# Eleven of the late units of a two-layer stage from one fp32 product to three fp32r products, with the low half made by VectorE out of PSUM

## The reference

```python
xm = x * cmask                                  # channels past a count are zero
h = gelu(einsum('bct,bch->bht', xm, W_sess[id]) + b_sess[id])     # 256 hidden
o = (einsum('bht,hs->bst', h, W2) + b2) * tmask                   # 128 out, masked in time
w_q = fp8_e4m3(weight * 448 / max|weight|)                        # 2048 x 2048
o_q = fp8_e5m2(o * 57344 / max|o|)
out = x + (o_q @ w_q.T) / scales + bias
```

## Time and profile before

| | |
|---|---|
| median of 3 runs | 832.65 us (832.58 to 834.17) |
| the profiled execution | 834.57 us, of which 832.8 us are the span of the profile |
| TensorE | 824.1 us busy, 99% of the span, 98% of the chain that ended last |
| VectorE / ScalarE / GpSimd | 479.5 / 345.8 / 511.8 us busy |
| granted TensorE clock | 1.00 |
| stage one ends, stage two starts | about 382 us after the start of the span |

### The profile page before, as it was taken

One profiled execution on the slowest core, in us unless ns is written; L12 is line 12 of the kernel. 1 busy time (PEld: TensorE's weight loads), 2 busy tenths in 40 slices (PEclk: granted clock), 3 DMA queues, 4 the chain that ended last, 5 costly groups with the idle time before them and its releaser, 6 DMA issues.

```text
span 832.8 us, 10134 instructions
## 1 busy us (share of the span) xinstructions
PE 824.1 (99%) x3521; PEld 481.6 (58%) x3568; DVE 479.5 (58%) x499; ACT 345.8 (42%) x372; POOL 511.8 (61%) x238
## 2 busy tenths in 40 slices
PE   9999999999999999999999999999999999999998
PEld 6777777776767676765444444444444444444444
DVE  5989899888888888888553333323232323232322
ACT  6899999988898888883200000000000000000000
POOL 2899999889999999995983242424242424232322
PEclk9999999999999999999999999999999999999999
DMA  7888999878777777656974768686868686868682
GB/s 257 300 324 311 387 322 348 307 283 305 298 270 301 302 289 287 249 202 230 308 293 124 272 219 279 212 281 210 283 214 282 212 281 213 283 214 280 213 251 107
DMA packets 75008, 220.77 MB, mean 265 GB/s; under 512 B 37594, under 2 KB 40930, under 8 KB 55778
## 3 DMA queue, kind: packets, MB, share of 16 engines
q1 hardware_dynamic: 74080, 219.30, 74.1%
q10 hardware_dynamic: 898, 1.09, 0.4%
HBM read 143.04 MB, written 69.21 MB: 255 GB/s over the span
## 4 chain that ended last, share of the span: by engine, by line
PE 98%; issue 0%; DMA 0%; DVE 0%; ACTq 0%; ACT 0%
PE ps_h L1071 53%; PE ps_h L980 22%; PE ps_o L995 11%; PE ps_o L1011 8%; PE ps_o L1007 4%; DMA counts_i<-in__lenS 0%; PE ps_h L1047 0%; PE ps_o L934 0%; PE ps_o L1071 0%; PE ps_o L980 0%; PE ps_o L940 0%; PE ps_o L1065 0%; ACTq L650 0%; PE ps_h L1052 0%; DVE o_and_max L881 0%
## 5 line engine op out<-in xcount | busy, mean ns | idle before, releaser
L1071 PE MATMUL ps_h<-wqT,x_sb 128*128 128x512 bf16 x1877 | 411.3, 378 | 2.4 <-ACT x_sb L702 0.2
L1071 PEld LDWEIGHTS ps_h<-wqT,x_sb 128*128 128x128 fp8e5 x1920 | 187.7, 98 | 224.4 <-ACT x_sb L702 0.3
L528 POOL TENSOR_TENSOR xl<-x_sb,xh 128x1024 fp32r<-128x1024 f32 x62 | 149.6, 2413 | 17.5 <-ACT xh L607 17.5
L980 PE MATMUL ps_h<-xh,whl 128*128 128x512 f32 x508 | 151.6, 419 | 0.4
L569 POOL TENSOR_TENSOR x_sb<-x_sb,bias_sb 128x2048 f32<-128x2048 f32 (+1 forms) x15 | 66.7, 4445 | 131.7 <-DMA x_sb<-in_x 131.7
L569 POOL TENSOR_TENSOR h<-h,bias_sb 128x2048 f32<-128x2048 f32 (+1 forms) x15 | 66.6, 4442 | 123.0 <-DMA h<-in_x 123.0
L881 DVE SCALAR_TENSOR_TENSOR o_and_max<-ps_h,scales,h 128x512 f32<-128x512 f32 (+1 forms) x59 | 44.0, 746 | 136.2 <-PE ps_h L1071 136.2
L881 DVE SCALAR_TENSOR_TENSOR o_and_max<-ps_h,scales,x_sb 128x512 f32<-128x512 f32 x59 | 44.2, 750 | 133.4 <-PE ps_h L1071 133.4
L980 PEld LDWEIGHTS ps_h<-xh,whl 128*128 128x128 f32 x508 | 95.0, 189 | 41.9 <-issue 21.9
L765 DVE SCALAR_TENSOR_TENSOR o_and_max<-ps_o,b_sb,steps 128x1024 f32<-128x1024 f32 (+1 forms) x65 | 82.2, 1264 | 29.0 <-PE ps_o L1011 27.2
L755 DVE TENSOR_TENSOR hl<-ps_h,hh 128x1024 fp32r<-128x1024 f32 x63 | 76.8, 1219 | 15.1 <-ACT ps_h L614 15.1
(11 more groups left out here) (101 smaller groups left out, 657.6 us busy)
## 6 DMA issues: line engine op xcount, KB each, us to landing
x_sb<-in_x SPq DMA_DIRECT2D x44, 1024.0 KB, 5.6
masked_out<-o_and_max SPq DMA_DIRECT2D x32, 1024.0 KB, 6.6
o_in<-masked_out SPq DMA_DIRECT2D x32, 1024.0 KB, 8.9
out<-o_and_max SPq DMA_DIRECT2D x27, 1024.0 KB, 5.1
wqT<-in_L_ffn_weight SPq DMA_DIRECT2D x23, 684.0 KB, 8.2
wt<-in_L_ffn_weight SPq DMA_DIRECT2D x40, 384.0 KB, 5.4
h<-in_x SPq DMA_DIRECT2D x14, 1024.0 KB, 7.2
whl<-split_w SPq DMA_DIRECT2D x18, 256.0 KB, 5.9
```

Of the source, the lines that this page charges most:

```text
L528: pool.tensor_tensor(xl[:, u % 2, :], x_cols(u), xh[:, u % 2, :].bitcast(fp32), ALU.subtract)\
L980: mm = nc.tensor.matmul(to[:, cols], whl[:, b % SLOTS_W, rows], xs[:, u % 2, cols], start=(k == 0), stop=(k == 2))
L1071: mm = nc.tensor.matmul(bank, q[:, k // 2, :, k % 2], wq[:, n, k, cols], start=(k == 0), stop=(k == KT - 1))
```

## The change

Unit 27 joins `SPLIT_H1`. Eleven units (30, 33, ... 60, `SPLIT_BEHIND`) get three fp32r products in `project1` in place of one fp32 product. ACT writes their high half to SBUF and the full gelu back into PSUM (in place of one gelu to SBUF), and DVE makes the low half out of `ps_h[:, 1, :]`, where the same work for units 2 to 27 is POOL's. The next `hidden(u+1, 1)` then waits for DVE too. `QUANT` becomes 27, so that 34 chunks are early and 9 late; the constants of chunk 34 are made in the last iterations of stage one, ACT scales chunk 36 ahead of the copies of the turned batch, and DVE's late chunks stand behind groups 2, 4, 5, 6 and 7 (before: 4, 5, 6, 7).

```diff
-    SPLIT_H1 = [u for u in range(2, 27)]
+    SPLIT_H1 = [u for u in range(2, 28)]
+
+    SPLIT_BEHIND = [u for u in range(30, UNITS - 2, 3)]
...
-    QUANT = SCANS + 2
+    QUANT = SCANS + 3
...
-    CHUNK_BEHIND = range(4, 12)
+    CHUNK_BEHIND = (2, 4, 5, 6, 7)
...
+        hh1_behind = sb_at("hh1_behind", [P, 2, UNIT], fp32r, h1_at)
+        hl1_behind = sb_at("hl1_behind", [P, UNIT], fp32r, raw_at)
...
-            for i in late[0:2]:
+            for i in late[0:3]:
                 round_chunk(i)
             pool.wait_ge(x2_loaded[1], 16)
             add_bias(x2[1], FRONT)
-            for i in late[2:6]:
+            for i in late[3:7]:
                 round_chunk(i)
...
+                if u in SPLIT_BEHIND:
+                    act.activation(hh1_behind[:, u % 2, :], ps_h[:, 1, :], ACT.Gelu, bias=hbias[:, 1, b:b + 1])
+                    act.activation(ps_h[:, 1, :], ps_h[:, 1, :], ACT.Gelu, bias=hbias[:, 1, b:b + 1])\
+                       .then_inc(h1_gelu, 1)
+                    return
...
+            scale_chunk(EARLY_CHUNKS + 2)
+
             for k in range(CUTS):
                 act.wait_ge(q_turned, k + 1)
...
+            def split_h1_behind(u):
+
+                dve.wait_ge(h1_gelu, u + 1)
+                if u == SPLIT_BEHIND[0]:
+                    dve.wait_ge(wl_later, DIRECT - UPB)
+                dve.tensor_tensor(hl1_behind[:, :], ps_h[:, 1, :], hh1_behind[:, u % 2, :].bitcast(fp32), ALU.subtract)\
+                   .then_inc(hl1_behind_ready, 1)
...
                     mask_o(u - 1, start, 0, slice(0, UNIT))
+                    if u in SPLIT_BEHIND:
+                        split_h1_behind(u)
...
+                if 0 <= u - QUANT - 1 < EARLY_CHUNKS:
+                    exponents(u - QUANT - 1)
                 if 0 <= u - QUANT - 1 < EARLY_CHUNKS + 1:
-                    exponents(u - QUANT - 1)
-                if 0 <= u - QUANT - 1 < EARLY_CHUNKS:
                     round_at(u - QUANT - 1)
                 if u + 1 < UNITS:
                     split_h_rest(u + 1)
+                if u - QUANT - 1 == EARLY_CHUNKS - 1:
+                    exponents(EARLY_CHUNKS)
...
             late = range(EARLY_CHUNKS, CHUNKS)
-            round_at(late[0])
             quantize(1, 1, True, slice(0, T))
...
                     pe.wait_ge(h1_gelu, u)
+                    if u - 1 in SPLIT_BEHIND:
+                        pe.wait_ge(hl1_behind_ready, SPLIT_BEHIND.index(u - 1) + 1)
...
+                elif u in SPLIT_BEHIND:
+
+                    for j, (w, hs) in enumerate(((w2l1, hh1_behind[:, u % 2, :]), (w2h1, hh1_behind[:, u % 2, :]),
+                                                 (w2h1, hl1_behind))):
+                        for cols in halves:
+                            mm = nc.tensor.matmul(ps_o[:, u % 2, cols], w[:, :], hs[:, cols],
+                                                  start=False, stop=(j == 2))
```

More of the change, by code:

```diff
@@ L126, in adaln_ffn @@
         x_sb = sb("x_sb", [P, 2, T], fp32)
+        raw_at = -(-nc.sbuf_base // 32) * 32
         raw = sb("raw", [P, SLOTS_W, HID], fp32)
+        assert SLOTS_W * HID == UNIT
         whl = sb("whl", [P, SLOTS_W, 2 * HID], fp32r)
@@ L137, in adaln_ffn @@
         hl = sb("hl", [P, 2, UNIT], fp32r)
+        h1_at = -(-nc.sbuf_base // 32) * 32
         h1 = sb("h1", [P, 2, UNIT], fp32)
@@ L236, in adaln_ffn @@
         hl1_ready = sem("hl1_ready")
+        hl1_behind_ready = sem("hl1_behind_ready")
         hl_ready = sem("hl_ready")
@@ L582, in _ @@
             add_bias(x2_more[0], FRONT)
-            for i in late[6:]:
+            for i in late[7:]:
                 round_chunk(i)
@@ L705, in _ @@
             for i in range(EARLY_CHUNKS + 2, CHUNKS):
-                scale_chunk(i)
+                if i > EARLY_CHUNKS + 2:
+                    scale_chunk(i)
                 if UNITS - QUANT + 2 <= i + 3 < CHUNKS:
@@ L902, in _ @@
                        .then_inc(y_ready, 1)
-                if y in CHUNK_BEHIND and 4 + CHUNK_BEHIND.index(y) < len(late):
+                if y in CHUNK_BEHIND:
                     i = late[4 + CHUNK_BEHIND.index(y)]
```

## The result

The changed kernel is slower: a ratio of 1.0098 to the kernel before, 95% interval 1.0086 to 1.011. Its six runs have a median of 842.6 us (840.43 to 842.76), the kernel before 833.48 (832.58 to 834.17) over six. The profiled execution took 842.63 us, against 834.57. The forecast was 841.2 us, with a range of 839 to 845.5.

The account below looks back on a forecast made before the run. PE's own sequence bounds the kernel, but in eleven units it would come to wait for DVE's `hl`: 8.9 - 0.34 = +8.6 us, from the 832.65 us median 841.2 us. Range 839 to 845.5 us, to hold 8 times in 10.

Parts of the forecast that it names:

- Which wait would end last: PE in the eleven units: the wait for `hl` decides; the new wait at `hidden(u+1, 1)` for the subtract lies inside it.
- The slack: DVE's chain to `hl` before the change: could end only 0.19 us later before delaying PE's next `hidden`.
- The addition: DVE's chain from `mask_o` to `hl`: the new subtract lengthens it by 1.02 us, at most 1.26.
- The restart: PE after a real wait: its xl group starts 0.15 + 1.00 = 1.15 us after `hl` ends.
- A unit: Each of the eleven units: PE's next xl group later by 0.83 us (odd) or 0.79 us (even), 8.9 us in all.
- PE's saving is inside the wait: `project1` of the eleven units: the 0.34 us saved by three products only brings PE to the wait sooner.
- Unit 27: Three products with POOL making the low half and no chunk worked on in that iteration: -0.34 us.
- The number: Whole kernel: +8.6 us, giving 843.1 us for an execution like the profiled one and 841.2 us from the 832.65 median.
- The late part: Late chunks after stage one: cost 0, or +3 us if the cover fails; ACT has 3.3 us before the first copy.
- The followed-forward times of POOL: POOL's late chunks in stage two: third `add_bias` forecast at about 415.2, before the change 415.05.
- The 3 us of cover: Stage two, group 6: DVE waits for POOL's third `add_bias`, PE wants that bank at about 422.4, slack 3 us.
- The rule on four passes of true fp32: Trainium skill's rule for PE's fp32 products: dropping one pass would save 0.43 us a unit, where the rows give 0.34.

Follow-up runs that it names:

- e_subtract_after_scan: Changed kernel with DVE's subtract behind scan_o instead of ahead of it: median 844.47 us, ratio 1.0136 to the kernel before.
- d_no_subtract: Changed kernel without the subtract and PE's wait for it, the third product taking the high half again: median 831.24 us, ratio 0.9964 to the kernel before.
- b_twice: Changed kernel plus a second DVE instruction of the subtract's size, an unread reduce, in the eleven units: median 855.02 us, ratio 1.025 to the kernel before.
- a_no_behind: Changed kernel with SPLIT_BEHIND empty, keeping unit 27 on three products, QUANT 27 and nine late chunks: ratio 0.9995 to the kernel before.
- c_fp32_product: Changed kernel with one fp32 product of the high half in the eleven units, low half made but left out: median 842.56 us, ratio 1.0098.
- f_scan_last: Changed kernel with scan_o behind split_h_rest from unit 29 on: median 833.19 us, ratio 0.9993 to the kernel before; 829.4 us was expected.
- h_scan_last_every2: Changed kernel with scan_o behind split_h_rest and every second unit from 30 (16, not 11) on three products: median 831.97 us, ratio 0.9977.
- j_no_subtract_scan_last: Changed kernel, scan_o behind split_h_rest except in stage one's last two iterations, no subtract or wait for it, high half counted again: median 828.63 us, ratio 0.9936.

## Why the prediction was right

- **Which wait would end last.** Forecast: PE waits for `hl` in each of the eleven units, and a wait of 0.15 us for the subtract lies inside that. Shown by the row of eleven waits, and by `e_subtract_after_scan`, where it takes a later subtract to make that the long one.
- **The slack.** Worked out as 0.19 us from rows in which no cost of a wait is to be seen. `d_no_subtract` bears it out from the other side: a unit with three products and the old chain gives 0.20 to 0.24 us of its 0.34. The trace of the kernel before holds a test of its own, in unit 53 (three rows of PE and one of DVE):

```profile
318.53 1.88 PE L1011 MATMUL ps_o<-h,w_sb 128*128 128x512 f32 x4
321.18 0.62 PE L980 MATMUL ps_h<-xl,whl 128*128 128x512 f32 x2
327.24 0.62 PE L980 MATMUL ps_h<-xl,whl 128*128 128x512 f32 x2
...
320.96 1.28 DVE L765 SCALAR_TENSOR_TENSOR o_and_max<-ps_o,b_sb,steps 128x1024 f32<-128x1024 f32 x1 [1.18 <-PE ps_o L1011]
```

  The mask starts 2.43 us after its product group, where rows 3 and 5 have 2.09 (200.72 to 202.81): 0.34 late. The unit takes 6.06 us instead of 5.89, so 0.17 of the 0.34 was slack. In `d_no_subtract`, where no slack is left, a mask as late (234.80 to 237.24, 2.44 us) costs all of it: that unit takes 6.05 us (237.45 to 243.50) instead of 5.69.
- **The addition.** 1.02 us forecast; mask to end of `hl` grew from 5.11 to 6.12 us, 1.01. `b_twice` adds 1.13 us for one more instruction, 1.14 expected.
- **The restart.** 0.15 + 1.00 us forecast from one early unit, 0.14 + 1.00 measured.
- **A unit.** Forecast +0.83 (odd) and +0.79 (even), measured 6.71 - 5.89 = +0.82 and 6.65 - 5.89 = +0.76. The sum of eleven was forecast as 8.9 us; it comes to 8.49 between the stretches of `a_no_behind` and the changed kernel, and to 8.7 from the eleven steps. The term was 2 to 5% too large.
- **PE's saving is inside the wait.** Shown by `c_fp32_product`, 842.56 us against 842.6.
- **Unit 27.** -0.34 us forecast, -0.36 in the stretch of `a_no_behind`.
- **The number.** The sum was +8.6 us; the two profiled executions differ by 842.63 - 834.57 = 8.06 us (the stretch by 8.13). That the median came out at 842.6 and not 841.2 is not the sum's doing, which was some 0.5 us too high. The forecast started from the median of three runs, 832.65; over six it is 833.48, and the last section shows why such medians wander by 1 to 2 us. The forecast for an execution like the profiled one, 843.1, is the one to compare: 842.63.
- **The late part.** Forecast at 0, measured 0.00 us. ACT's copy of the first turned batch came 3.36 us after it was free, 3.3 forecast:

```profile
390.24 0.94 ACT L647 ACTIVATE ws<-wt,scales 128x768 f32<-128x768 f32 x1 [1.99 <-POOL wqT L546]
394.53 0.69 ACT L718 ACTIVATE x_sb<-ps_o 128x256 fp8e5<-128x256 f32 x2 [3.36 <-PE ps_o L1102]
```

  The followed-forward times of POOL were less exact. Its third `add_bias` was forecast 0.15 us later than before (415.05); it started at 423.88, which is 0.8 us later once the 8.06 us are taken off by which stage two starts later (384.66 to 392.72), and DVE's group 6 came at 427.41, 0.8 us later likewise. The 3 us of cover took that.
- **A miss outside the prediction.** Of my expectations, that of `f_scan_last` failed. The prediction had said that the wait at `hidden(u+1, 1)` lies inside the other, and had worked out 0.15 us for it. When the other is gone it stands alone, and I had left it out of the 829.4 us. With it (11 x 0.17 = 1.9 us) and the 0.65 us of the end the forecast for the stretch would have been 4.1 - 1.9 - 0.65 = 1.55 us shorter than before; it was 1.39. `h_scan_last_every2` missed by the same omission.

The rule on four passes of true fp32 (the Trainium skill, "FP8 and Floating Point Precision", section TensorE Precision Notes) would make three products worth 0.43 us a unit, by the prediction's estimate (1.72 / 4). The traces have 0.34 for unit 27 and 0.32 to 0.33 in `j_no_subtract_scan_last`, where PE is not held up, near what rows 3 and 4 gave; the measured number decides.

## What to carry to other kernels

Idle time of an engine is spendable only on the side of the wait where it lies. DVE was idle for 0.7 us in every unit, but behind the instruction that PE waits for; what counted was the 0.2 us between the end of that instruction and the moment PE would feel it. So before work is given to an engine that is 58% busy, follow its chain from the event that starts it to the event that another engine waits for, and put what nobody waits for (here a maximum) behind that event. The Trainium skill, "Perfetto Trace Analysis", section Optimizing Scalar/DVE Operations, says that breaking up instructions may help where VectorE isn't saturated but causes bubbles on other engines. No run here breaks one up; here the order alone took the loss away (a ratio of 0.9993 to the kernel before in place of 1.0098).

When a long wait is removed, the shorter one that it covered comes out at its full price: price it ahead, from the same timeline.

## What the runs showed that I had not expected

The runs of most kernels fall into groups 1 to 2 us apart (the changed kernel: 840.43 and 840.57, and four from 842.57 to 842.76). The traces show where: in the first 12 us. In the kernel before, PE's second group of xh products starts at 10.39 and its first groups are slow; in `a_no_behind`, which is the same program there, the same group starts at 8.68.

The timeline of the kernel before:

```profile
6.81 2.07 PE L934 MATMUL ps_o<-time 128*128 128x256 f32 x4
8.32 1.42 PE L980 MATMUL ps_h<-xh,whl 128*128 128x512 f32 x2
```

and of `a_no_behind`:

```profile
6.52 1.13 PE L962 MATMUL ps_o<-time 128*128 128x256 f32 x4
7.64 0.74 PE L1010 MATMUL ps_h<-xh,whl 128*128 128x512 f32 x2
```

The same matmuls take about twice as long (1.42 and 0.74 us for two). The granted clock in these stretches reads 1.00 in both traces. But in `c_fp32_product` and `j_no_subtract_scan_last` matmuls are slow a little later, from about 8.5 to 11.8 us, and there it is down. In the timeline of `j_no_subtract_scan_last`:

```profile
8.46 1.05 PE L1009 MATMUL ps_h<-xl,whl 128*128 128x512 f32 x2
9.31 1.91 PE L1009 MATMUL ps_h<-xh,whl 128*128 128x512 f32 x4
```

and the busy times of its engines from 10 to 11 us, where the third number from the end is the granted clock:

```profile
10.00:11.00 1.00, 1.00 (x3) 0.74 (x3) 1.00 (x1) 0.53 (x1) 0.00 (x0) 0.50 1.01 256
```

That is the lower of the clock's two levels (1.2 and 2.4 GHz). The xl group of two takes 1.05 us there, and 1.05 us at 9.54 in the kernel before too. So the clock is the likely cause in the kernel before as well, with its fall missing from that trace; this is argued and not shown. PE's wait just ahead doesn't tell the kinds apart: 0.60 us in the kernel before and 0.86 us in `j_no_subtract_scan_last`, which turn slow, and 0.93 us in `a_no_behind`, which doesn't. The 1.8 us between the first and the last are still there at the group of `hidden(27, 0)` (162.48 and 160.68). No experiment was made on it. It is why differences under 2 us are read here from the stretch and not from the medians.
